# Transformer layer on one core: early loads spread over FFN blocks, one Q wait per bank, value products three tiles behind

## What is computed

```python
xn = layernorm(x)                                   # x: 2 x 1024 x 512, float32
q = xn @ Wq.T                                       # 32 heads of 128
k_r, c = xn @ Wkr.T, xn @ Wdk.T                     # rotated part of the keys, latent of keys and values
k_c, v = c @ Wupk.T, c @ Wupv.T                     # 8 kv heads; 4 q heads share one
q, k_r = rope(q), rope(k_r)
p = softmax(causal(q @ k.T / sqrt(128)))
out = x + (p @ v) @ Wo.T + (silu(xn @ Wg.T) * (xn @ Wu.T)) @ Wd.T   # FFN, 1792 wide
```

## Time and profile before

| | before |
|---|---|
| median of 3 runs | 2465.45 us (2463.36 to 2466.46) |
| profiled execution | 2469.72 us, span 2467.5 us |
| TensorE matmul busy | 2366.8 us, 96% |
| TensorE weight load busy | 1975.6 us, 80% |
| VectorE, ScalarE, GpSimd busy | 60%, 46%, 38% |
| granted TensorE clock, mean | 0.988 |
| keys part | 0 to 609 us |
| opening and attention | 609 to 2467 us |

### The profile page before, as it was taken

The page is one execution under the profiler, slowest core; times in us unless marked ns, Lnnn a source line. Parts: engine busy times, 40 slices in busy tenths (PEclk is TensorE's granted clock), DMA queues, the critical chain, the costliest instruction groups (busy, mean ns, idle before and its releaser), DMA issues.

```text
span 2467.5 us, 38965 instructions
## 1 busy us (share of the span) xinstructions
PE 2366.8 (96%) x11840; PEld 1975.6 (80%) x11840; DVE 1483.8 (60%) x3641; ACT 1134.6 (46%) x2217; POOL 939.7 (38%) x813
## 2 busy tenths in 40 slices
PE   6999999989899999999999999999999999999998
PEld 5777877768688888878887888788888878888886
DVE  4343334424576666766676767666666666676765
ACT  2442624335354544444454545354545444454544
POOL 1000000000454444545454545455444545454543
PEclk9999999999999999999999999999999999999999
DMA  5676757788312121231313152312222121213110
GB/s 191 188 285 184 257 168 247 266 274 286 131 49 98 44 96 63 83 104 36 104 43 104 35 192 84 119 44 95 67 81 95 43 104 44 103 35 112 35 52 18
DMA packets 103736, 287.26 MB, mean 116 GB/s; under 512 B 9056, under 2 KB 42336, under 8 KB 92512
## 3 DMA queue, kind: packets, MB, share of 16 engines
q1 hardware_dynamic: 101408, 280.53, 33.9%
q10 hardware_dynamic: 2112, 4.19, 0.4%
HBM read 200.80 MB, written 83.89 MB: 115 GB/s over the span
## 4 chain that ended last, share of the span: by engine, by line
PE 63%; issue 7%; DVE 3%; ACT 3%; DMA 2%; POOL 2%; SPq 1%; ACTq 0%; DVEq 0%; POOLq 0%
PE qb L1113 14%; PE ob L1153 14%; PE ob L1168 13%; PE scores L1131 12%; PE ptb L1142 9%; DMA ff_raw<-in_ffw 2%; DVE pT L1065 1%; ACT pT L1018 1%; PE ring L874 1%; POOL prob L979 1%; SPq L601 1%; ACT prob L1005 1%; SPq L608 0%; POOL late_qT L989 0%; POOL q_cos L985 0%
## 5 line engine op out<-in xcount | busy, mean ns | idle before, releaser
L979 POOL TENSOR_TENSOR prob<-prob,rinv 128x896 f32<-128x896 f32 (+7 forms) x512 | 583.2, 1149 | 407.4 <-DVE rinv L1083 405.8
L1018 ACT ACTIVATE pT<-ptb 128x512 fp32r<-128x512 f32 x576 | 335.9, 594 | 568.7 <-PE ptb L1142 561.9
L1005 ACT ACTIVATE prob<-prob,nmax 128x896 f32<-128x896 f32 (+7 forms) x512 | 396.2, 774 | 329.5 <-DVE nmax L1044 324.2
L1153 PE MATMUL ob<-pT,v_sb 128*128 128x512 f32 x1728 | 509.4, 413 | 13.6 <-DVE pT L1065 11.1
L1065 DVE TENSOR_TENSOR pT<-ptb,pT 128x512 fp32r<-128x512 f32 x576 | 390.9, 688 | 126.6 <-ACT pT L1018 119.8
L1044 DVE CUSTOM_DVE_ANT_0 prob<-scores,mask 128x896 f32<-128x896 f32 (+7 forms) x512 | 384.6, 753 | 44.6 <-issue 30.5
L985 POOL TENSOR_TENSOR q_cos<-q_cos,q_sin 128x512 f32<-128x512 f32 x125 | 161.8, 1294 | 563.9 <-DVE q_cos L1061 563.9
L1113 PE MATMUL qb<-xT,wq 128*128 128x512 f32 x1500 | 362.6, 391 | 5.2 <-DVE q_cos L1061 3.6
L1153 PEld LDWEIGHTS ob<-pT,v_sb 128*128 128x128 f32 x1728 | 297.9, 190 | 83.8 <-DVE pT L1065 42.4
L1142 PE MATMUL ptb<-ident,prob 128*128 128x128 f32 x2304 | 341.9, 275 | 7.2 <-POOL prob L979 6.5
L1131 PE MATMUL scores<-kT,late_qT 128*128 128x448 f32 (+3 forms) x1536 | 339.5, 356 | 1.4
(11 more groups left out here) (86 smaller groups left out, 2254.0 us busy)
## 6 DMA issues: line engine op xcount, KB each, us to landing
wq<-w_parts SPq DMA_DIRECT2D x126, 512.0 KB, 3.8
w_parts<-stage SPq DMA_DIRECT2D x32, 1024.0 KB, 4.9
ff_raw<-in_ffw SPq DMA_DIRECT2D x56, 384.0 KB, 3.8
k_parts<-stage SPq DMA_DIRECT2D x128, 128.0 KB, 2.4
v_parts<-stage SPq DMA_DIRECT2D x64, 256.0 KB, 3.6
w_raw<-in_wqo SPq DMA_DIRECT2D x32, 512.0 KB, 6.0
kT<-k_parts SPq DMA_DIRECT2D x16, 1024.0 KB, 7.1
v_sb<-v_parts SPq DMA_DIRECT2D x16, 1024.0 KB, 9.0
```

Of the source, the lines that this page charges most:

```text
L979: nc.gpsimd.tensor_tensor(prob[:, n % 2, h, 0:W], prob[:, n % 2, h, 0:W], rinv[:, hd % 8:hd % 8 + 1].broadcast_to([P, W]), ALU.mult)\
L1005: nc.scalar.activation(prob[:, n % 2, j, 0:W], prob[:, n % 2, j, 0:W], ACT.Exp, bias=nmax[:, hd % 8:hd % 8 + 1], scale=-1.0, accum_out=rsu ...
L1018: nc.scalar.activation(pT[:, t % 3, HI], ptb[t % 2][:], ACT.Copy).then_inc(pT_hi, 1)
L1153: mm = nc.tensor.matmul(ob[:], v_sb[e % 2][:, x, j], pT[:, t % 3, y], start=(j == 0 and (x, y) == (HI, HI)), stop=(is_last(kind, n, j) and ...
```

## The change

The early loads are placed anew. Of x only chunk 0 is loaded where it was. V of head 0 goes out in FFN block 2 of the last chunk, the two Wq parts in block 3, the first half of Wo in block 4, the two halves of the second x chunk in blocks 5 and 6, and the second half of Wo in the last block behind the opening Wq parts. In the opening the fifth and sixth Q product use the first and second of the four banks and wait only for the reading of that bank; VectorE's turn of the fifth waits only for the first split. The first value product waits until the sixth Q bank is read. Value products stand three tiles behind the transposes; for that `pT` has four slots instead of three, and to make room `prob` for even units holds only 6 key blocks, so that the 7-block unit must be an odd one: `ORDER` swaps query blocks 5 and 6. The planner writes the orders of the other engines for the new row of products.

```diff
+SHORT = 6 * P
-ORDER = (3, 2, 1, 0, 4, 5, 6, 7)
+ORDER = (3, 2, 1, 0, 4, 6, 5, 7)
-LAG = 2
+LAG = 3
-        pT = sb("pT", 3 * KB, [P, 3, 2, 512], F32R)
-        oT = sb("oT", 15 * KB, [P, 2, 512], F32R)
-        prob = sb("prob", 19 * KB, [P, 2, GRP, S])
+        pT = sb("pT", 3 * KB, [P, 4, 2, 512], F32R)
+        oT = sb("oT", 19 * KB, [P, 2, 512], F32R)
+        prob = [sb("short_prob", 23 * KB, [P, GRP, SHORT]), sb("long_prob", 35 * KB, [P, GRP, S])]
+        def query_bank(n, opening):
+
+            if opening and n < AHEAD + EARLY:
+                return first_qb[n % AHEAD]
+            return qb
-        def early_values(sp):
-            sp.wait_ge(emptied, CHUNKS * GROUPS + G_V)
-            load_v(sp, 0)
-            for p in range(2):
-                sp.wait_ge(w_kept[p], 8 * SPLIT_BLOCKS * 3)
-            load_wq(sp, 0)
-            load_wq(sp, 1)
-
-        def early_weights(sp, m):
+        def early_rest(sp, m):
             if m == 2:
                 sp.wait_ge(emptied, (CHUNKS + 1) * GROUPS)
+                for p in range(2):
+                    sp.wait_ge(w_kept[p], 8 * SPLIT_BLOCKS * 3)
+                load_v(sp, 0)
+            elif m == 3:
+                load_wq(sp, 0)
+                load_wq(sp, 1)
+            elif m == 4:
                 load_wo_a(sp, 0)
-            elif m == 3:
-                load_wo_b(sp, 0)
+            elif m in (5, 6):
+                sp.dma_start(x2T[:, 1, m - 5].bitcast(F32).rearrange("p k s -> p (k s)"),
+                             scr["xT"][1, :, m - 5].rearrange("p k s -> p (k s)")).then_inc(opening_loaded, 16)
             elif m == MB - 1:
                 for h in range(2):
                     sp.dma_start(opening_wq[:, h].bitcast(F32).rearrange("p x k d -> p (x k d)"),
                                  scr["w"][1, :, h].rearrange("p x d -> p (x d)")).then_inc(opening_loaded, 16)
+                load_wo_b(sp, 0)
-            sp.wait_ge(opening_loaded, 32)
+            sp.wait_ge(opening_loaded, 64)
             for x in range(2):
                 sp.sem_inc(wq_loaded[x], 16)
+            sp.sem_inc(x_ready[1], 16)
-                if last:
-                    early_x(sp, 1)
...
                         if opening and n == 0 and j == 0:
                             act.wait_ge(ff_stored, 16 * (CHUNKS + 1))
                             act.wait_ge(w_kept_lo, SPLIT_BLOCKS * (CHUNKS + 1))
+                            for p in range(2):
+                                act.wait_ge(w_kept[p], 8 * SPLIT_BLOCKS * (CHUNKS + 1))
...
                         if not opening or n >= AHEAD:
-                            dve.wait_ge(q_split, it1 * UNITS + n)
+                            dve.wait_ge(q_split, it1 * UNITS + (1 if opening and n == AHEAD else n))
...
                         if not opening or n >= AHEAD:
-                            pe.wait_ge(q_read, it1 * UNITS + n)
-                        bank = first_qb[n] if opening and n < AHEAD else qb
+                            pe.wait_ge(q_read, it1 * UNITS + (n if not opening else n - AHEAD + 1))
+                        bank = query_bank(n, opening)
...
+                        if opening and n == 0 and j == 0:
+                            pe.wait_ge(q_read, it1 * UNITS + AHEAD + EARLY)
```

More of the change, by code:

```diff
@@ L497, in same_batch, with early_x @@
                 sp.sem_inc(s, 16 * (PAIRS - 1))
+        def query_bank(n, opening):
+            if opening and n < AHEAD + EARLY:
+                return first_qb[n % AHEAD]
+            return qb
         def turning(n, opening):
             if opening and 0 < n < AHEAD:
-                return prob[:, 1, n, 0:512], prob[:, 1, n, 512:1024]
+                return prob[1][:, n, 0:512], prob[1][:, n, 512:1024]
             return q_cos[:], q_sin[:]
-        def early_x(sp, x):
-            c1 = CHUNKS
-            sp.wait_ge(emptied, c1 * GROUPS + (G_CT if x == 0 else G_KR))
+        def early_x(sp):
+            sp.wait_ge(emptied, CHUNKS * GROUPS + G_CT)
             sp.wait_ge(xT_stored, 16 * 3)
-            load_queries_x(sp, 0, x)
+            load_queries_x(sp, 0, 0)
         def early_keys(sp):
@@ L585, in chunk @@
                 if last:
-                    early_x(sp, 0)
+                    early_x(sp)
                 if not last:
@@ L592, in chunk @@
                         early_keys(sp)
-                    if last and n == G_V:
-                        early_values(sp)
                     sp.wait_ge(emptied, c1 * GROUPS + n + 1)
@@ L624, in chunk @@
                     if last:
-                        early_weights(sp, m)
+                        early_rest(sp, m)
             load_x(0)
@@ L1004, in work @@
                         act.wait_ge(inv_ready, it1 * HPB + hd - 7)
-                        nc.scalar.activation(prob[:, n % 2, j, 0:W], prob[:, n % 2, j, 0:W], ACT.Exp,
+                        nc.scalar.activation(prob[n % 2][:, j, 0:W], prob[n % 2][:, j, 0:W], ACT.Exp,
                                              bias=nmax[:, hd % 8:hd % 8 + 1], scale=-1.0,
@@ L1044, in work @@
                         nc.vector.tensor_tensor_reduce(
-                            prob[:, n % 2, j, 0:W].rearrange("p (a c) -> p a c", a=parts),
+                            prob[n % 2][:, j, 0:W].rearrange("p (a c) -> p a c", a=parts),
                             scores[hd % 2][:, 0:parts * 512].rearrange("p (a c) -> p a c", a=parts)[:, :, 0:W // parts],
@@ L1104, in work @@
                             w_q = opening_wq[:, n - 2]
-                            pe.wait_ge(opening_loaded, 32)
+                            pe.wait_ge(opening_loaded, 64)
                         else:
@@ L1142, in work @@
                             mm = nc.tensor.transpose(ptb[t % 2][:, h * P:(h + 1) * P],
-                                                     prob[:, n % 2, h, j * P:(j + 1) * P], ident[:])
+                                                     prob[n % 2][:, h, j * P:(j + 1) * P], ident[:])
                         mm.then_inc(t_done, 1)
@@ L1152, in work @@
                         for x, y in PASSES:
-                            mm = nc.tensor.matmul(ob[:], v_sb[e % 2][:, x, j], pT[:, t % 3, y],
+                            mm = nc.tensor.matmul(ob[:], v_sb[e % 2][:, x, j], pT[:, t % 4, y],
                                                   start=(j == 0 and (x, y) == (HI, HI)),
```

6 lines of the change are left out of this document (3 added, 3 removed).

## The result

The changed kernel takes **2448.02 us** (median of 4 runs, 2445.25 to 2450.46) against 2464.40 us (2462.93 to 2466.46) of the kernel before beside it: ratio 0.9933, 95% interval 0.9919 to 0.9947, or -16.4 us. The forecast was 2447.3 us, -18.1 us. The profiled execution took 2448.94 us, span 2446.7 us, 20.8 us shorter than that of before. So this pair of profiles flatters the change by some 4 us; where, the part on the sum of the loops says.

The account below looks back on a forecast made before the run. TensorE works through nearly the whole span, so only its waits or slowdowns matter. Terms -6.1 - 2.7 - 15.8 + 6.8 - 0.3 = -18.1 us take the median from 2465.45 to 2447.3 us, range 2438 to 2463.

Parts of the forecast that it names:

- Value stage: Last chunk, before the first FFN block: without V and Wq loads ahead, stores start earlier, gaining 6.6 us.
- FFN stage: Last chunk: loads beside FFN blocks cost 0 (0 to +2); 0.5 us given back for block 2's cast.
- rival B: Transfers decide: value stores stay slow (-3), blocks 5 and 6 cost 2, opening gains nothing; 2455.1 us, chance 0.20.
- net of the loads: Last chunk, value stage gain less the cast wait given back: -6.1 us (-3 to -7.5).
- Opening: Start of attention: the chain through GpSimd to the first transpose moves earlier, -2.7 us (0 to -5).
- Long units: Units with 6 to 8 key blocks: last product's wait goes, 0.99 us a run, 16 runs, -15.8 us (-12 to -17).
- swapped order: Loops, 7 key blocks before 6: same total work, norms still in time, cost 0 (0 to +5).
- rival A: Long units: the last product's wait isn't a loss or only moves; sum -2.3 us, 2463.2 us, chance 0.10.
- 4-block unit: Third transpose (number 3) waits for VectorE's split, 0.45 us lost in each of fifteen units, +6.8 us (+2 to +9).
- Sum of the loops: Loops and end: -15.8 for long units, +6.8 for 4-block units, -0.3 at the end, together -9.3 us.
- C: 8-block unit: last head's norm comes late, 16 us per us beyond 0.2; 2468.1 us at 1.5 us, chance 0.07.
- second way: Last chunk's value stage: the wait becomes chunk 3's, 8.90 - 3.05 = 5.85 us gained.

Follow-up runs that it names:

- e3: Kernel before with only the loads placed as in the change (V, Wq, Wo, x1 in FFN blocks): 2460.53 us, ratio 0.9975.
- e5: Changed kernel with V and the first two Wq loads put back ahead of the value stores: 2452.11 us, ratio 0.9955.
- e11: The changed kernel again, unaltered, in a later call: 2448.91 us, ratio 0.9925.
- e6: Changed kernel, but value products only two tiles behind in units of up to 4 key blocks: 2441.19 us, ratio 0.9907.
- e7: Changed kernel with the residual's load of x behind the FFN weights of block 2 in every chunk: 2441.30 us, ratio 0.9911.
- e1: Kernel before with only the opening's waits and Q banks changed: 2461.59 us, ratio 0.9978.
- e2: Kernel before with only value products three tiles behind, the unit order and the two buffer sizes: 2456.99 us, ratio 0.9964.
- e9: Kernel before with only the unit order changed, 7 key blocks ahead of 6: 2468.74 us, ratio 1.0005.
- e10: Kernel before with only the residual's load of x moved behind the FFN weights of block 2: 2461.30 us, ratio 0.9978.
- e4: Changed kernel with the second x chunk loaded at the last chunk's start again, not in blocks 5 and 6: 2444.12 us, ratio 0.9917.

## Why the prediction held, and the step of it that failed

**Value stage: the mechanism and nearly the size.** Forecast 6.6 us, from stores that start earlier and issue at chunk 3's pace. They issued in 13.58 us, the wait fell to 1.58 us (2 to 3.5 was announced), and the stage fell by 7.4 us in e3, with the same 11.2 us for its first projection as before. In the first profile of after it is 5.7 us, as that projection took 12.80 us, partly at 1.2 GHz (granted clock 0.86). The K and table loads, whose part I left open down to half, stayed ahead of the stores in every run, so at most the 1.58 us that are left can be theirs; e5 puts back V and Wq alone and has the whole wait.

**FFN stage: the step that failed.** I wrote 0 (0 to +2) for the loads beside FFN blocks and 0.5 for block 2's cast. The stage gave back 5.8 us, in e11 5.1 us, and in e6, whose keys part is the same, 3.7 us. The cast cost block 2 waits of 1.79, 1.90 and 1.44 us in them, and in the first two another 1.6 us by the clock. The shorter wait ahead of the stage had also freed the first pair of blocks from 1.66 us of low clock (9.22 to 7.56), which I hadn't counted; without that the first profile would have given back 7.5 us. One edit takes 6.9 us of the stage away again (e7, 84.89 to 77.96). The fault was to read the 362 GB/s window of the earlier trace rows as the answer to "do the bytes fit". They do fit (e7). What mattered is when one small load lands, and that went by what stood ahead of it on the queue: the FFN weights of 0.38 MB have to be there for a cast one block ahead. Two windows of the changed kernel fit this:

```profile
556.00:562.00 6.00, 5.21 (x23) 3.86 (x23) 2.52 (x3) 4.04 (x7) 0.00 (x0) 1.00 0.88 333
562.00:568.00 6.00, 6.00 (x27) 4.71 (x26) 2.52 (x3) 3.60 (x6) 0.00 (x0) 1.00 1.01 341
```

TensorE lacks 0.79 us in the window with the less busy DMA, and nothing in the one at 1.01. The right cost was in sight: the earlier trace rows had a cast wait in chunk 3, and the residual load stood ahead of it in the code. With the stall gone, the delay of block 2 that it had covered in the last chunk came back.

A second part isn't block 2's. e5 has the stall and block 2 in time, and its FFN stage is still 3.7 us longer than before, with 2.4 us of waits for hT in four places and x1 in blocks 5 and 6. That is rival B's term. e7 has the same loads in blocks 5 and 6 and one such wait of 0.37 us. So these waits too went when the residual was moved; which load made them in e5 isn't shown.

The net of the loads is -4.6 us in e3's profile (-6.2 by its ratio), between the forecast's -6.1 and its bound of -3; in the two profiles of the full change both stages together differ from before by +0.15 and -0.6 us, and that holds 1.6 us of low clock in the first projection and 1.6 at block 2 in each; without these it would be -3.0 and -3.8 us.

**Opening: right.** The split of Q 4 was to end at 632.2 us with the first Q product at 609.15, 23.05 us after it. It ended at 628.42 + 1.26 = 629.68 us, 23.03 us after 606.65. The first transpose came 2.76 us earlier against the first Q product; forecast 2.7. TensorE's own wait of 3.62 us would have been the wrong number, as the forecast said. The other 2.9 us of this stretch are the clock, and luck: they lie between the first transpose and the first score product of unit 2, which took 8.94 us before at a granted clock of 0.54 and 6.05 us after at 0.99. e1 and e6, with the same edit, took 7.94 and 8.05 us at 0.66 and 0.65. The forecast had left this open with 2 us either way.

**Long units: right.** 0.99 us a run was forecast and 1.02 measured (e6), although the swapped order inside it costs 0.09. A loop body of two runs goes down by 1.06 us with the 4-block price in it, as announced (1.0). The nine matmuls of 2.62 us became twelve of 3.02, where 2.62 + 0.69 would have been 3.31 with the wait in place; from their start to that of the next Q product it is 2.86 us, where before it was 2.46 (from 1204.57 us to the line below) and 0.69 more would be 3.15:

```profile
1207.03 2.90 PE L1113 MATMUL qb<-xT,wq 128*128 128x512 f32 x12
```

Either way 0.29 us are gone, and rival A is refuted. The weight-load wait of 0.45 us would have given half again too much; the difference of the starts was the right reading. The Trainium skill, in "Perfetto Trace Analysis", section Identifying the Most-Contended Engine, says that matmul busy time is no good measure and has the busy share of the weight loads (with the share of peak work) read instead. Here it was the waits in the weight-load row that found the place, and the wait's length overstated the price.

**4-block unit: right.** 0.45 us forecast, 0.49 measured (e6 against after), where the matmul row shows [0.29].

**Sum of the loops.** 16 x 0.53 = 8.5 us, forecast 9.3, e2 8.9. The profiled stretch fell by 12.6 us, and that isn't one lucky pair: the five profiles with two tiles (before, e1, e3, e9, e10) have 1812.1 to 1818.0 us from the first score product of unit 2 to the end, the six with three tiles throughout (after, e2, e4, e5, e7, e11) 1802.2 to 1804.8, in the mean 11.6 us less. The mean granted clock doesn't tell them apart: it is 0.988 both in the kernel before and in e2, which has 1804.0 us. So some 3 us more than the counted waits are gone, and the forecast missed them. They lie in the runs of eight Q products over a turn of the loop, which fell by 1.0 us each (116.99 to 115.96, mean of six), not 0.53; what waits there I didn't trace.

The profile pair differs by 20.8 us and the medians by 16.4. The 2.9 us of the opening and the -2.6 us ahead of the last chunk, where nothing was changed, are what flatters it: the same 1841 matmuls there were busy for 421.78 us before and 418.86 after. Over the ten profiles without the residual edit this stretch varied from 458.64 to 464.17 us.

**Rivals.** C: no transpose waits for GpSimd in a loop body, and in the 8-block unit the first transpose follows the score without a gap, 0.68 us behind it. The norm was over at 1179.98 us and the transpose started at 1180.90, 0.9 us to spare where the forecast left 0.2. B had the right sign for the FFN stage, but put it on blocks 5 and 6 and at 2 us, where block 2 was the larger part; its other two terms, slow stores and an opening without gain, are refuted. The mechanisms held in four places of five, but that the median came out at 2448.0, 0.7 us from 2447.3, is luck: the FFN stage lost some 5 us more than forecast, and against that stand a value stage up to 0.8 us better, some 3 us more in the loops, and the turns of the clock. The three parts alone sum to -5.4 - 8.9 - 6.2 = -20.5 us, the whole change was timed at -16.4 (13.1 to 20.0) and in e11 at -18.5 us: the single terms are known to some 1 us, the sum by timing only to 3.

## What to carry over

A stall can cover delays behind it: when it is taken away, follow each engine from its end and ask of each small load what now stands ahead of it on its queue; that the bytes fit into the time doesn't say that the one needed next comes first. A pipeline distance should be a property of the unit, not of the kernel: three tiles behind pays where a product would wait for its own tile, and costs where two transposes then stand together. To size a wait in the middle of matmuls, take the difference of the starts over a fixed group, and best over a whole period.

## What the runs showed of the hardware that I had not expected

- A wait of 8.3 to 8.9 us of TensorE was followed by a stretch at 1.2 GHz in all six profiles that have it, and one of 1.6 to 1.7 us at the same place in none of seven: 1.7 to 2.5 us that belong to the price of the wait and stand in no wait row. Chunks 2 and 3 show it at 3.0 to 3.3 us of wait, in all 13 profiles (8.88 to 9.18 us for the same 32 matmuls), so that a wait like chunk 3's, which the forecast took as its second way, would have kept the low clock. Block 2 doesn't follow its own wait so plainly: its 16 matmuls took 5.5 us after waits of 1.79 and 1.90 us in the two profiles of the changed kernel, but 3.92 us after 2.10 us (e3) and 2.06 us (e4), and 3.93 after 1.44 (e6). What decides there stays open.
- Taking the residual's load off the way of block 2's weights saved 5.4 us in the kernel before (ratio 0.9978; 5.7 us by the three stages of the profiles, 1.6 of them the clock) where the matmul row showed 1.64 us of cast waits in the ordinary chunks.
- One core's DMA moved 346 GB/s over 78 us, at a share of 0.97, beside a TensorE that was busy for 77.39 of them, and 406 GB/s over 10 us of the opening.
